# A layernorm, recurrence and expert kernel: the skip term made on chip, clears on another queue, ScalarE's work in another order

## What is computed

```python
xn = _layernorm(x, axis=-1)
s = _L0_attn_ref(xn, ...)
g = _silu(_L0_ffn_ref(xn, ...))
x = x + s * g

dt = soft_clamp(softplus(x @ Wdt.T + bdt), 0.001, 0.1, 0.5)
B_param = x @ WB.T;  C_param = x @ WC.T
A = -exp(soft_clamp(A_log, -5.0, 5.0, 0.5))
dA = exp(soft_clamp(dt[..., None] * A, -8.0, 8.0, 0.5))
dB = dt[..., None] * B_param[:, :, None, :]
def step(h, inp):
    dAt, dBt, xt, Ct = inp
    h = dAt * h + dBt * xt[..., None]
    h_norm = sqrt(sum(h * h, axis=(1, 2)))
    h = h * minimum(20.0 / (h_norm + 1e-08), 1.0)
    y = einsum('bdn,bn->bd', h, Ct) + Dp * xt
    return h, y

h = gelu(einsum('ecd,edf->ecf', exp_batches, c_fc))
exp_out = einsum('ecf,efd->ecd', h, c_proj)
out = cb_weight @ exp_out
```

## Time and profile before

| | before |
|---|---|
| runs, us | 1703.8, 1704.61, 1704.99 (median 1704.61) |
| the profiled execution, us | 1704.6, its span 1702.6 |
| PE busy | 1291.1 us, 76% of the span |
| DVE busy | 1549.6 us, 91% |
| ACT busy | 1225.1 us, 72% |
| POOL busy | 770.4 us, 45% |
| granted TensorE clock, mean | 0.867 |
| DMA, mean | 67 GB/s |

### The profile page before, as it was taken

One profiled execution on the slowest core, in us unless ns is written; L12 is line 12 of the kernel. 1 busy time (PEld: TensorE's weight loads), 2 busy tenths in 40 slices (PEclk: granted clock), 3 DMA queues, 4 the chain that ended last, 5 costly groups with the idle time before them and its releaser, 6 DMA issues.

```text
span 1702.6 us, 33871 instructions
## 1 busy us (share of the span) xinstructions
PE 1291.1 (76%) x9356; PEld 1136.9 (67%) x9356; DVE 1549.6 (91%) x9454; ACT 1225.1 (72%) x3152; POOL 770.4 (45%) x1254
## 2 busy tenths in 40 slices
PE   5864435297979797997979798897979798855661
PEld 5753324286868686886868687796878687744551
DVE  6688888899999999998999899999989999987778
ACT  3697548278787887868787887878787777756451
POOL 3156666543434344343444344343434434468842
PEclk8576767698989899998989999898989899877785
DMA  9931111210111021021002002011101110012245
GB/s 332 340 127 47 44 41 44 95 36 17 51 49 46 17 77 31 18 62 50 28 24 86 24 26 75 25 39 37 63 18 34 66 32 20 20 44 71 75 127 202
DMA packets 95533, 113.29 MB, mean 67 GB/s; under 512 B 8432, under 2 KB 85360, under 8 KB 95344
## 3 DMA queue, kind: packets, MB, share of 16 engines
q1 hardware_dynamic: 87696, 94.13, 17.0%
q0 software_dynamic: 6144, 16.79, 3.1%
q10 hardware_dynamic: 1504, 0.22, 0.1%
HBM read 60.91 MB, written 50.20 MB: 65 GB/s over the span
## 4 chain that ended last, share of the span: by engine, by line
PE 54%; DVE 14%; ACT 12%; issue 7%; POOL 7%; DMA 4%; SPq 1%; POOLq 0%; ACTq 0%; DVEq 0%
PE ps L1210 15%; PE ps L1194 13%; PE ps L1182 10%; PE ps L1176 6%; ACT arena L870 4%; POOL arena L531 4%; DVE arena L751 3%; POOL xg L511 3%; PE ps L1141 3%; PE ps L1157 3%; DVE arena L722 2%; DVE arena L728 2%; DVE arena L740 2%; DVE arena L736 2%; ACT arena L858 2%
## 5 line engine op out<-in xcount | busy, mean ns | idle before, releaser
L531 POOL TENSOR_TENSOR arena<-arena,neghalf 128x1 f32<-128x1 f32 x1025 | 591.8, 577 | 851.2 <-DVE arena L725 780.3
L751 DVE SCALAR_TENSOR_TENSOR arena<-arena 128x128 f32<-128x128 f32 x1024 | 361.6, 353 | 54.0 <-POOL arena L531 53.6
L1182 PE MATMUL ps<-arena,pick 128*128 128x128 f32 x2048 | 301.9, 294 | 38.8 <-ACT arena L966 19.8
L736 DVE CUSTOM_DVE_ANT_0 arena<-arena 128x128 f32<-128x128 f32 x1024 | 294.0, 287 | 30.3 <-ACT arena L966 25.4
L1176 PE MATMUL ps<-ident,arena 128*128 128x128 f32 x1024 | 210.7, 333 | 137.6 <-ACT arena L870 132.0
L966 ACT ACTIVATE arena<-ps,arena 128x128 f32<-128x128 f32 x1024 | 291.4, 376 | 32.8 <-PE ps L1182 32.8
L1182 PEld LDWEIGHTS ps<-arena,pick 128*128 128x128 f32 x2048 | 280.2, 211 | 50.9 <-ACT arena L966 38.0
L1194 PE MATMUL ps<-arena,wf 128*128 128x256 f32 x1280 | 302.0, 386 | 8.1 <-issue 8.1
L728 DVE CUSTOM_DVE_ANT_0 arena<-arena 128x128 f32<-128x128 f32 x1024 | 299.0, 292 | 0.0
L1210 PE MATMUL ps<-wp,arena 128*128 128x256 f32 x1280 | 295.8, 385 | 2.6 <-ACT arena L974 2.3
L1176 PEld LDWEIGHTS ps<-ident,arena 128*128 128x128 f32 x1024 | 179.9, 244 | 167.4 <-ACT arena L870 137.2
(11 more groups left out here) (146 smaller groups left out, 1379.7 us busy)
## 6 DMA issues: line engine op xcount, KB each, us to landing
xg<-zeros SPq DMA_DIRECT2D x10, 1024.0 KB, 9.6
xrow<-xg SPq DMA_DIRECT2D x40, 256.0 KB, 2.7
yg<-arena SPq DMA_DIRECT2D x40, 256.0 KB, 2.2
arena<-in_x SPq DMA_DIRECT2D x16, 512.0 KB, 9.3
wf<-in_c_fc SPq DMA_DIRECT2D x8, 1024.0 KB, 5.0
wp<-in_c_proj SPq DMA_DIRECT2D x8, 1024.0 KB, 6.0
arena<-dx SPq DMA_DIRECT2D x66, 64.0 KB, 2.4
ys<-arena SPq DMA_DIRECT2D x66, 64.0 KB
```

The lines of the kernel that those rows point to most:

```text
L531: g.tensor_tensor(sv[:, slot, 1:2], mx, neghalf[:, 0:1], ALU.pow).then_inc(s_ready, 1)
L736: v.tensor_tensor_reduce(out=junk[:, 1, :], in0=vv, in1=vv, scale=1.0 / CLAMP ** 2, scalar=0.0, op0=ALU.mult, op1=ALU.add, accum_out=ac[:, ...
L751: v.scalar_tensor_tensor(hr[:, slot, :], vv, sv[:, before, 1:2], ur[:, slot, :], ALU.mult, ALU.add)\
L1182: last = t.matmul(ps[2][:, j * P:(j + 1) * P], pick[:, q * QUAD + j, :], xin, start=True, stop=True)
```

## The change

**The skip term.** The tensor `dx` in memory goes, with DVE's eight products, the eight writes, four small clears of its padding and the 66 loads. D is loaded as two columns (`dcol`), and ACT makes D times the normalised input of a half on chip by two operations, `skip_of(h)`. The first matmul of `output(n)` took the loaded piece against the identity; now it takes the skip piece against the identity. Outputs 0 and 1, which belong to no real block, have no such matmul.

**The clears.** The ten clears of `xg` are issued by POOL, after its eight rstd operations and ahead of three memsets that the recurrence needs.

**The order on ACT and PE.** Time rates and `logs_of` go from the last quad of a half and its end to the second quad of the next; `b_and_c` with its evictions goes a block later, from the second quad of the first block to that of the second; sums of squares from the second block's first quad to the third's; `squares_of`, now with `skip_of`, from the end of the first block to the end of the second. DVE's product for the sums follows a block later.

```diff
-            for b in range(NB):
-                sp.dma_start(dx[0:YPAD, b, :], zeros[0:YPAD, 0:D]).then_inc(padz, 16)
-            def clear(i):
-                sp.dma_start(xg[i * NT:(i + 1) * NT, :].rearrange("(r p) d -> p r d", p=P),
-                             zeros[:, 0:D].unsqueeze(1).broadcast_to([P, CH, D])).then_inc(moe_zero, 16)
...
-                sp.wait_ge(dxn_ready, i + 1)
-                sp.dma_start(dx_tok[:, i], dxn[:, i % 2]).then_inc(dx_done[i % 2], 16)
...
-                if blk > 0:
-                    load_dx(blk, span(blk * BLK, BLK))
...
+                    if i >= 3:
+                        sp.wait_ge(skip_ready, 2 * (i - 1))
...
+            for i in range(SLOTS // NT):
+                g.dma_start(xg[i * NT:(i + 1) * NT, :].rearrange("(r p) d -> p r d", p=P),
+                            zeros[:, 0:D].unsqueeze(1).broadcast_to([P, CH, D])).then_inc(moe_zero, 16)
...
-                v.tensor_tensor(dxn[:, i % 2, :, :], xnat[:, :, i, :], dpb.unsqueeze(1).broadcast_to([P, NB, D]),
-                                ALU.mult).then_inc(dxn_ready, 1)
...
+            def skip_of(h):
+                if h >= 2:
+                    act.wait_ge(y_done, 4 * h - 1)
+                for k in range(DH):
+                    last = a.activation(skip[:, h % 2].rearrange("p (t b k) -> p k b t", b=NB, k=DH)[:, k], source(h)[:, k], ACT.Copy,
+                                        scale=dcol[:, k:k + 1])
+                last.then_inc(skip_ready, 1)
...
+            skip_of(0)
+            skip_of(1)
...
-                    if blk % 4 == 0 and blk > 0 and q == 1 and blk // 4 + 2 < HALVES:
+                    if blk % 4 == 1 and q == 1 and blk // 4 + 2 < HALVES:
                         b_and_c_out(blk // 4 + 2, 6)
-                    if blk % 4 == 1 and q == 0 and 2 <= blk // 4 + 1 < HALVES:
+                    if blk % 4 == 2 and q == 0 and 2 <= blk // 4 + 1 < HALVES:
                         sums_out(blk // 4 + 1, 6)
...
+                    if blk % 4 == 0 and q == 1 and blk // 4 + 2 < HALVES:
+                        logs_of(blk // 4 + 2, 6)
-                if blk % 4 == 3 and blk + 4 < NBLK:
-                    if (blk + 9) // 4 < HALVES:
-                        logs_of((blk + 9) // 4, 6)
...
-                if blk % 4 == 0 and 2 <= blk // 4 + 1 < HALVES:
+                if blk % 4 == 1 and 2 <= blk // 4 + 1 < HALVES:
                     squares_of(blk // 4 + 1)
+                    skip_of(blk // 4 + 1)
...
-                pe.wait_ge(dx_in, (n + 1) * 16)
-                t.matmul(ps[3][:, 0:P], ident[:, :], dxt, start=True, stop=False)
+                if n >= 2:
+                    h, at = divmod(n - 2, 4)
+                    pe.wait_ge(skip_ready, h + 1)
+                    t.matmul(ps[3][:, 0:P], skip[:, h % 2, at * P:(at + 1) * P], ident[:, :], start=True, stop=False)
...
-                    h = {(3, 3): blk // 4 + 3, (0, 1): blk // 4 + 2, (1, 0): blk // 4 + 1}.get((blk % 4, q), 0)
+                    h = {(0, 1): blk // 4 + 2, (1, 1): blk // 4 + 2, (2, 0): blk // 4 + 1}.get((blk % 4, q), 0)
```

More of the change, by code:

```diff
@@ L69, in build @@
         xts = nc.dram_tensor("xts", (CH, P, DH, NB, P), f32, kind="Internal").ap()
-        dx = nc.dram_tensor("dx", (NT + YPAD, NB, D), f32, kind="Internal").ap()
         ys = nc.dram_tensor("ys", (NT + YPAD, NB, D), f32, kind="Internal").ap()
@@ L84, in build @@
         a16c = sb("a16c", [P, DH * NS])
+        dcol = sb("dcol", [P, DH])
         be = sb("be", [P, NT, 2])
@@ L90, in build @@
         slot_of = sb("slot_of", [P, 2, TILES], i32)
-        ARENA = 40816
+        ARENA = 41712
         arena = sb("arena", [P, ARENA])
@@ L116, in build @@
         xin = take(P)
-        dxt = take(P)
+        skip = take(2 * SD).rearrange("p (f s) -> p f s", f=2)
         vv = take(P)
@@ L147, in lay @@
             return arena[:, at2[0] - n:at2[0]]
-        dxn = wf.rearrange("p k f -> p (k f)").rearrange("p (f b d) -> p f b d", f=2, b=NB)
         wg_sb = lay(DH * NE).rearrange("p (k m) -> p k m", k=DH)
-        dpb = lay(D)
         stats = lay(2 * NB * 6).rearrange("p (f b s) -> p f b s", f=2, b=NB)
@@ L225, in build @@
         xch_in = [sem(f"xch_in{k}") for k in range(2)]
-        dxn_ready = sem("dxn_ready")
-        dx_done = [sem(f"dx_done{k}") for k in range(2)]
+        skip_ready = sem("skip_ready")
         lg_ps = sem("lg_ps")
@@ L328, in build @@
         for h in range(2, HALVES):
-            for table, pieces, lo_, hi_ in ((sum_at, 1, 4 * h - 8, 4 * h - 6), (input_at, 2, 4 * h - 5, 4 * h - 3), (norm_at, 1, 4 * h - 2, 4 * h)):
+            for table, pieces, lo_, hi_ in ((sum_at, 1, 4 * h - 7, 4 * h - 5), (input_at, 2, 4 * h - 5, 4 * h - 3), (norm_at, 1, 4 * h - 2, 4 * h)):
                 lo_, hi_ = max(lo_ * BLK + 3, BLK + 2), max(hi_ * BLK, 2 * BLK)
@@ L350, in _ @@
             sp.dma_start(yg[SLOTS:SLOTS + P, :], zeros[:, 0:D]).then_inc(padz, 16)
-            for b in range(NB):
-                sp.dma_start(dx[0:YPAD, b, :], zeros[0:YPAD, 0:D]).then_inc(padz, 16)
-            def clear(i):
-                sp.dma_start(xg[i * NT:(i + 1) * NT, :].rearrange("(r p) d -> p r d", p=P),
-                             zeros[:, 0:D].unsqueeze(1).broadcast_to([P, CH, D])).then_inc(moe_zero, 16)
             for i in range(CH):
-                clear(i)
                 sp.wait_ge(xn_ready, i + 1)
                 sp.dma_start(xnd.rearrange("(b i p) d -> p b i d", p=P, i=CH)[:, :, i, :], xnat[:, :, i, :]).then_inc(xn_out, 16)
-                sp.wait_ge(dxn_ready, i + 1)
-                sp.dma_start(dx_tok[:, i], dxn[:, i % 2]).then_inc(dx_done[i % 2], 16)
                 if i >= 1:
@@ L376, in load_rows @@
                 sp.dma_start(home, xnd[first * P:(first + count) * P, :].rearrange("(j p) d -> p j d", p=P)).then_inc(tile_in[n], 16)
-            sp.wait_ge(padz, 16 * (NB + 1))
+            sp.wait_ge(padz, 16)
             sp.sem_inc(y_out, 1)
-            sp.dma_start(dxt, dx[0:BLK, :, :].rearrange("t b (k d) -> (t b k) d", k=DH)).then_inc(dx_in, 16)
-            for i in range(CH, SLOTS // NT):
-                clear(i)
-            for k in range(2):
-                sp.wait_ge(dx_done[k], 16 * CH // 2)
             sp.wait_ge(xn_out, 16 * CH)
@@ L544, in _ @@
                     if n == 0:
+                        pool.wait_ge(memz, 1)
                         pool.wait_ge(moe_zero, 16 * (SLOTS // NT))
@@ L550, in _ @@
                     if n == 0:
-                        pool.wait_ge(padz, 16 * (NB + 1))
+                        pool.wait_ge(padz, 16)
                         pool.wait_ge(ye_out, 16 * NE * TPE)
@@ L795, in _ @@
             act.dma_start(bdt_sb, bdt.rearrange("(k p) -> p k", p=P), allow_slow_non_contiguous=True).then_inc(ld_v, 16)
-            act.wait_ge(ld_v, 32)
+            act.dma_start(dcol[:, :], dpar.rearrange("(k p) -> p k", p=P), allow_slow_non_contiguous=True).then_inc(ld_v, 16)
+            act.wait_ge(ld_v, 48)
             act.wait_ge(consts, CONSTS)
@@ L1142, in output @@
                                         win[:, step, QUAD - 1 - j:2 * QUAD - 1 - j, :].rearrange("p c g -> p (c g)"),
-                                        hr[:, half * BLK + step, :], start=False, stop=j == QUAD - 1)
+                                        hr[:, half * BLK + step, :], start=n < 2 and j == 0, stop=j == QUAD - 1)
                 last.then_inc(y_done, 1)
@@ L1221, in _ @@
                         after_evictions()
-                        if blk % 4 == 3 or (blk == 0 and q == 1):
+                        if blk % 4 == 0:
                             pe.wait_ge(xch_in[h // 2 % 2], 16 * ((h // 2 + 1) // 2))
@@ L1225, in _ @@
                             waiting = [z_used, h + 1]
-                        elif blk % 4 == 0:
+                        elif blk % 4 == 1:
                             b_and_c(h, 6)
```

21 lines of the change are left out of this document (removed).

## The result

The changed kernel takes 1759.03 us (median of four runs, 1756.58 to 1760.43) against 1704.8 us for the kernel before: a ratio of 1.0315, 95% interval 1.0297 to 1.0333. It is slower, as forecast, and by 54 us where 24.8 were forecast. The profiled execution after has a span of 1758.1 us, 55.5 more than the 1702.6 before.

The account below looks back on a forecast made before the run. PE's work and waits were taken to set the expert stage's length, with DVE trailing. The terms -3.7 + 1.8 + 15.2 + 4.9 + 6 + 4 - 5.6 + 2.2 sum to +24.8, so 1729.4 us, range 1712 to 1748.

Parts of the forecast that it names:

- The bound: Stage with the expert products: PE's work and waits add up to its length, 95.8 us per half, and DVE trails.
- Clearing on POOL's queue: Before the scan: ten clears hidden in POOL's 26.29 us idle time, priced at nothing; 64 us late at eight times the price.
- Start: Before the scan: removed DVE products gain 2.0 us and less memory writing 1.7, together -3.7 us.
- (a) Decays and time rates: Half boundaries: earlier decays win 15.6 us of ACT's idle time, moved time rates take back 17.4, so +1.8 us.
- (b) The wait of the selections: Each half's first block: PE's selection matmuls wait for ACT's input term behind the moved logarithms, +15.2 us, bounds zero and 30.
- Gelu, up and down: Fourth quad behind the moved lump: a down waits 0.9 to 1.1 us for Gelu, an up 1.0 for its bank; +4.9.
- The next block's inputs: Behind the moved lump: ACT evicts the next block's inputs late, 12.2 us by the walk, half taken: +6.
- (c) and relief: Squares and skip products ahead of a half's third block delay windows, +4 us; boundary and line 1072 waits go, -5.6.
- DVE's need: Third quad's terms, block 52: DVE needs them at 18.8 us after the restart and has them at 21.0, +2.2.
- The signs named beforehand: Expert stage: input-term waits over 12 us, decay stalls 9 to 10, DVE waits some 45, 71 table loads, halves about 98.
- the two marks for the start: First scan step: later than 81 us behind the clears means wrong; before 76 means the start was worth more.

Follow-up runs that it names:

- 5: Changed kernel with 3 to 9 unread matmuls keeping PE busy in the new waits for the input term, eight blocks: 1752.44 us, ratio 1.0275.
- 11: Changed kernel with 18 unread matmuls in each of the twelve stalls for the decays: 1735.75 us, ratio 1.0194.
- 6: Kernel before the change with 18 unread matmuls in each of the twelve stalls for the decays: 1701.47 us, ratio 0.9976.
- experiment 3: Changed kernel with the ten clears back on SP's queue, spread between the chunks: 1754.44 us, ratio 1.0274.
- 4: Changed kernel with one activation table holding both Exp and Ln loaded ahead of the logarithms, 62 loads instead of 71: 1746.08 us, ratio 1.0231.
- 8: Changed kernel with old order and clears on SP's queue, plus 18 unread matmuls in each of twelve decay stalls: 1694.15 us, ratio 0.9936.
- 9: Changed kernel with old order and clears on SP's queue, only the logarithms moved behind the first quad's input term: 1693.95 us, ratio 0.9945.
- 10: Old order, clears on SP's queue, logarithms behind first quad's input term, plus 18 unread matmuls in each of twelve decay stalls: 1683.72 us, ratio 0.9881.

## Why the prediction was right in its direction and wrong in its size

- **The bound.** That PE's work and waits add up to the stage holds for the new order (5 and 11). For the old order it was half the truth: 6 shows that ACT's logarithms and windows were as late as PE there. "The logarithms lie behind a stall that PE has anyway" is right, and the slow first quad is part of what hid them. The prediction read that quad's slowness (2.19 us for an "up" against 1.89 later in block 36 of the kernel before) nowhere as clock, though the granted clock from 971.5 to 976.4 was 0.67:

```profile
974.17 2.19 PE L1194 MATMUL ps<-arena,wf 128*128 128x256 f32 x8
```

- **Clearing on POOL's queue.** Right that it is hidden: 0.92 us each, under the 1.13 of the nearest row. What was costed at nothing and is not: the transfers. They cost 5 to 12 us at the 17th step (10.7 in the pair of experiment 3). DVE worked in only 3.55 of the 9.3 us of issuing, so what a busy DVE would do to such issues is not shown.
- **Start.** -3.7 forecast, +2.0 measured at block 12, but the three other executions of the same start (4, 5, 11) were there 1.0 to 3.5 us before the kernel before; so the sign is not settled. The gain of the removed products was underestimated (6 to 10 at step 17), and the bunch took it back.
- **(a) Decays and time rates.** +1.8 forecast. The stalls grew from 107.9 to 112.9: +5.0. ACT's idle time ahead of the inputs was won in part (31.0 to 17.1 us in the stage), but the down's eviction now stands in the stall.
- **(b) The wait of the selections.** +15.2 forecast, 1.6 to 20.9 measured: +19.3. Piece by piece the walk holds: 1.62 for 1.25 (blocks 12, 16, 28, 40), 2.86 for 2.55 (24, 36), 4.43 for 4.2 (44), 0.68 for 0.85 (48); block 52, with 1.62, was left out of the sum. Each of these lengths was within 0.4 us.
- **Gelu, up and down.** +4.9 forecast; 2.3 to 4.1 and nothing to 1.5 measured, +3.3.
- **The next block's inputs.** The walk gave 12.2 and I took half, 6. Measured +9.7 in this stretch (9.3 to 19.0), with pieces of 3.0, 3.0, 2.8, 1.8 and 1.0 behind blocks 28, 40, 48, 52 and 20, 11.6 together: loads did not overlap, and halving was wrong. That the walk's whole sum fits is in part luck: 32 and 44, which it had, show no such wait, and 52, which it had not, does.
- **(c) and relief.** -1.6 forecast for both. The waits for windows, for row turns' evictions and for the sums went from 9.5 to 14.0: +4.5. The two waits for windows of 1.53 (blocks 18 and 30) are the 1.3 of the walk, and the 0.9 in 46 did not come; the 7.3 us of the sums of squares behind a row turn (L1057) were not seen.
- **DVE's need.** +2.2 forecast; it is not a term beside PE's, and no run shows it by itself.
- **The step that failed: the sum has no term for PE's clock.** Every product behind a new wait was priced as if nothing had happened ahead of it. Measured: +18.6 us of busy time, of which 1.8 are the extra time rates and 15.8 the clock's by its records, 8 to 9 of them shown by an experiment (5). The rest of the gap is the waits, which were sized too small: 40.2 measured against 26.3 in the sum, most of it in (c) with the relief (6.1 too low), in (b) (4.1) and in the next block's inputs (3.7). That start and end together (+2.0, -5.4) come near the start that was forecast (-3.7) is luck: no change of the end was forecast.
- **The signs named beforehand** came as told: waits for the input term over 12 us in the first block's fourth quad, stalls of 9 to 10, 71 loads, DVE's new waits at the eighth step. DVE's waits rose further, to 72.8 instead of 45, and a half takes 101.4 us on average (1115.9 / 11) instead of 98. The first step at 78.12 lay between the two marks for the start.

## What to carry to other kernels

A piece of work that is moved out of an engine's stall into the open can cost its length as a wait elsewhere, and for TensorE often slower products behind that wait besides: look in the profile at how the same product is priced right behind a wait and later, and count both. Two engines that are late by nearly the same amount hide each other: an edit to one alone then shows nothing (6, 8, 9), and only both together do (10). Transfers that are cheap to issue are not cheap to have in flight at once: spread them between those that somebody waits for.

## What the runs showed of the hardware that was not expected

A wait of 2.86 us and one of 0.75 just after it were enough for the granted clock to fall: 16 passes took 6.64 us behind them, and 3.72 with PE kept busy through the first wait. Behind a wait of 1.62 alone they took 3.62 (block 16). Ten DMAs of 1 MB on POOL's queue took 0.92 us each to issue and had a median of 22.6 us to landing; spread over SP's queue 9.3.
